# Two expert layers whose first nine slots are written among the routing of the last 20 tiles

## The chip, the cores and the metric

The kernel runs on one core of one Trainium2 chip. The metric is the device time in microseconds of one execution, taken as the median of several. TensorE does products and turns (transposes), VectorE, ScalarE and GpSimd the elementwise work, SyncE issues most transfers. A pass is one weight load with its stream: a product in f32 is recorded as two of them.

## What is computed

4096 tokens of width 256 (4 sequences of 1024) go through two layers. The part that matters here is the first layer:

```python
x = x + 0.5 * _L0_ffn_ref(_layernorm(x, axis=-1), ...)     # experts, first time
x = x + _L0_attn_ref(_layernorm(x, axis=-1), ...)          # causal attention, 16 heads of 16
x = x + 0.5 * _L0_ffn_ref(_layernorm(x, axis=-1), ...)     # experts, second time
x = x + 0.5 * _L1_ffn_ref(...)                             # block-wise quantized feed-forward
x = x + _L1_attn_ref(...)                                  # linear attention
x = x + 0.5 * _L1_ffn_ref(...)

def _L0_ffn_ref(hidden_states, W_router, W1, b1, Wo, bo, ln_gamma, ln_beta):
    logits = x @ W_router                                  # 4 experts
    expert_idx = jnp.argmax(logits, axis=-1)               # each token takes one
    h = gelu(jnp.einsum('th,ehi->tei', x, W1) + b1)        # 256 -> 1024
    intermediate = jnp.einsum('te,tei->ti', onehot, h)
    y = intermediate @ Wo + bo + x                         # 1024 -> 256
    return _layer_norm(y, ln_gamma, ln_beta)
```

## The kernel before

**Tiles and slots.** The tokens stand in 32 tiles of 128 rows. So that a token meets one expert alone, each layer of experts first routes: it normalizes all tiles, finds each token's expert, and scatters the tokens into `sorted_x` in DRAM, one region of rows for each expert. The experts then work on slots of 128 rows of one region; 35 slots (`SLOTS` = 32 + 3) hold any division of the tokens. A table says for each slot which expert it has (`expert_of`) and which row it starts at (`row_of`); SyncE and VectorE read it as registers. Results go to `sorted_y` and are gathered back tile by tile.

**Phases.** `build` (L2163) runs setup, `route_phase` (r0), `expert_qkv_phase`, `attention_phase`, `route_phase` (r1) and `second_layer_phase` one after the other, each with its own block and an all-engine barrier at its end. r1 also does the output projection of attention ahead of the norm; its fp4 weights are loaded meanwhile.

**Routing** (`route_phase`, L254). Stages are written as `(step, stage, every)`: stage k of tile t is issued at step t + k, in the same order on every engine, all unrolled. For tile t: turn_y L479 and project L486 (r1 only), join L329 on VectorE adds the projection to X; for four tiles measure L340 to L348; GpSimd takes the root L462; take_shift L355; ScalarE normalizes L437; TensorE turns L494; ScalarE evacuates L443; TensorE's router L503 gives four logits; choose L371 to L381 on VectorE, for four tiles; count_up L514 to L522; put L390 to L394; GpSimd scatters one tile with an indirect transfer L468. Banks of PSUM: two each for turned tiles, logits and projections. After tile 31 the table of slots is made by turns between TensorE (L534 to L547) and VectorE (L403 to L423).

**Experts** (`experts`, L556). One step is one slot. SyncE: load L603 (slice of sorted_x), load_weights L608 (1 MB of w1), load_residual L612, store L616 (waits for the finished slot). TensorE: 14 warm-up products L156, then turn L632, up_proj L641, down_proj L650 of three slots in a row, into two banks for the turn, two pairs of banks for up, two banks for down. ScalarE: evacuate L660, eight Gelus L671. VectorE: quantize_weights L1338 to L1423 (in the second layer, 18 pieces, one a slot, turned by TensorE at L1430), take_bias L682, place_results L717 to L741 (once, 25 linked steps, gives the rows for the gather), finish L690 to L172, norm L188 of the slot before. GpSimd: root L754, scale L761 and L762, gather L776.

**What follows the experts.** In the first layer `queries_keys_values` (L799) is interleaved with them, in the second the feed-forward stage (L1472) and the rest. `interleave` (L99) merges parts by their place; events at the same place keep the order of the parts and then of the stages. All waits are explicit semaphores.

## Time and profile before

| | us |
|---|---|
| median of 3 runs (2191.99 to 2197.48) | 2192.93 |
| the profiled execution | 2192.66 |
| its span, first to last instruction | 2190.9 |
| TensorE busy | 2043.9 (93%) |
| VectorE busy | 1455.5 (66%) |
| ScalarE busy | 1020.9 (47%) |
| GpSimd busy | 923.1 (42%) |

The profile is of one execution. Matmuls are pipelined and their ends are modelled, so that a start of the next one says more than a duration. A row `x32 3.74` is 32 instructions joined. What stands in brackets behind a row is the idle time ahead of it on its engine and what ended it. PE is TensorE, PEld its weight loads, DVE VectorE, ACT ScalarE, POOL GpSimd, SPq SyncE's queue.

### The profile page before, as it was taken

Reading aid. Unit: us, or ns where it says so; the run is one execution under the profiler, and the core shown is the slowest. Engines: PE = TensorE matmul, PEld = TensorE weight load, DVE = VectorE, ACT = ScalarE, POOL = GpSimd, SP = SyncE. Lnnn points to the kernel's source line nnn. Section 1 sums busy time; section 2 is a strip of 40 time slices with the busy share of each in tenths; the row PEclk is TensorE's granted clock in tenths of the full one; section 3 lists DMA queues with packets and bytes.
Section 4 is the critical chain, followed back from the end, with each engine's and each line's share of the span. In section 5 each row is a group of like instructions: output and inputs, shape, how many; then the busy total and the mean of one; then the engine's idle time right before and its main releaser. Section 6 shows DMA issues by size and latency. Waiting matters only on the chain.

```text
span 2190.9 us, 41818 instructions
## 1 busy us (share of the span) xinstructions
PE 2043.9 (93%) x13713; PEld 1408.7 (64%) x13713; DVE 1455.5 (66%) x3982; ACT 1020.9 (47%) x2367; POOL 923.1 (42%) x1137
## 2 busy tenths in 40 slices
PE   6799999989999999978899998999989999799998
PEld 6688887534444444347798885666766666566676
DVE  5344345478888888626675248889866666588884
ACT  4333333426666666645333333333346666533332
POOL 5334445412111111216134346555546666455553
PEclk9999999969999999998999999999999999999999
DMA  5456663563344444111556652000000000000000
GB/s 172 153 197 208 212 208 122 156 99 48 48 58 59 60 58 50 13 41 71 177 199 206 211 193 61 1 0 0 1 1 2 2 2 2 1 10 10 19 20 19
DMA packets 101710, 173.57 MB, mean 79 GB/s; under 512 B 14705, under 2 KB 66321, under 8 KB 101521
## 3 DMA queue, kind: packets, MB, share of 16 engines
q1 hardware_dynamic: 95376, 154.40, 26.7%
q0 software_dynamic: 6144, 16.79, 2.5%
q8 instruction: 102, 1.67, 0.3%
q14 instruction: 88, 0.71, 0.1%
HBM read 136.01 MB, written 34.87 MB: 78 GB/s over the span
## 4 chain that ended last, share of the span: by engine, by line
PE 23%; issue 10%; DVE 10%; POOL 6%; ACT 2%; DVEq 0%; POOLq 0%; DMA 0%; ACTq 0%; SPq 0%
PE s_H L1645 6%; PE s_Y L1675 4%; PE s_H L1997 3%; PE s_H L1984 1%; DVE ff_hscale L1358 1%; PE s_TY L2032 1%; PE s_Y L2068 1%; PE s_Y L2076 1%; PE s_H L2018 1%; DVE fw_down L1361 1%; DVE s_H L1538 1%; POOL V L776 1%; POOL fw_down L1588 1%; POOL e_yo L761 1%; POOL e_rstd L754 1%
## 5 line engine op out<-in xcount | busy, mean ns | idle before, releaser
L1253 DVE TENSOR_REDUCE a_part_max<-a_psS 128x1 f32<-128x512 f32 (+3 forms) x608 | 362.6, 654 | 78.0 <-PE a_psS L1183 69.2
L1309 ACT ACTIVATE a_PT<-a_psE 128x512 f32<-128x512 f32 (+1 forms) x608 | 309.3, 583 | 177.6 <-PE a_psE L1197 160.7
L1158 POOL TENSOR_SCALAR_AFFINE_SELECT a_PT<-a_PT 128x512 f32<-128x512 f32 x128 | 81.5, 636 | 407.7 <-ACT a_PT L1309 407.7
L1177 PE MATMUL a_psS<-sk,sq 96*128 96x512 bf16 (+3 forms) x768 | 234.4, 342 | 11.9 <-DMA sk<-qk_parts 8.1
L1197 PE MATMUL a_psE<-sq,sk 98*128 98x512 bf16 (+3 forms) x768 | 224.6, 329 | 2.5 <-ACT a_PT L1309 1.4
L1588 POOL TENSOR_TENSOR fw_down<-fw_down,ff_hm 128x704 f32<-128x704 f32 x64 | 97.3, 1521 | 248.1 <-DVE fw_down L1370 248.1
L1675 PE MATMUL s_Y<-w_down,fw_up 128*128 128x256 f32 x768 | 181.0, 386 | 20.9 <-ACT fw_up L1625 19.2
L754 POOL TENSOR_TENSOR e_rstd<-e_moments,minus_half 128x1 f32<-128x1 f32 x70 | 45.5, 649 | 333.5 <-DVE e_moments L172 333.5
L1610 ACT ACTIVATE ff_hm<-fw_down 128x704 bf16<-128x704 f32 x64 | 50.6, 790 | 280.3 <-DVE fw_down L1361 280.3
L1675 PEld LDWEIGHTS s_Y<-w_down,fw_up 128*128 128x128 f32 x768 | 143.5, 191 | 46.1 <-ACT fw_up L1625 29.0
L1645 PE MATMUL s_H<-w_gate,ff_xqT 128*128 128x512 f32 (+1 forms) x512 | 165.4, 467 | 3.0 <-ACT ff_sil L1620 3.0
L1645 PE MATMUL s_H<-w_up,ff_xqT 128*128 128x512 f32 (+1 forms) x512 | 164.2, 464 | 3.6 <-DVE fw_down L1361 2.4
L1197 PEld LDWEIGHTS a_psE<-sq,sk 98*128 98x128 bf16 x768 | 70.6, 98 | 131.7 <-issue 50.4
L1213 PE MATMUL a_psO<-a_PT,a_va 128*32 128x512 f32 (+3 forms) x1536 | 150.4, 494 | 2.5 <-POOL a_PT L1158 1.8
L1645 PEld LDWEIGHTS s_H<-w_gate,ff_xqT 128*128 128x128 f32 x512 | 90.2, 193 | 66.5 <-issue 66.4
L1645 PEld LDWEIGHTS s_H<-w_up,ff_xqT 128*128 128x128 f32 x512 | 89.6, 192 | 66.6 <-issue 61.9
L641 PE MATMUL eq_H<-e_xsT,e_w 128*128 128x128 f32 x1120 | 130.8, 275 | 0.0
L641 PE MATMUL s_H<-e_xsT,e_w 128*128 128x128 f32 x1120 | 130.8, 275 | 0.0
L1177 PEld LDWEIGHTS a_psS<-sk,sq 96*128 96x128 bf16 x768 | 73.0, 99 | 89.2 <-DVE a_part_max L1253 52.0
L641 PEld LDWEIGHTS eq_H<-e_xsT,e_w 128*128 128x128 f32 x1120 | 127.9, 192 | 0.1
L641 PEld LDWEIGHTS s_H<-e_xsT,e_w 128*128 128x128 f32 x1120 | 127.9, 192 | 0.1
L650 PE MATMUL eq_Y<-wo_moe,e_gT 128*128 128x256 f32 x560 | 126.7, 379 | 0.0
(374 smaller groups left out, 4314.8 us busy)
## 6 DMA issues: line engine op xcount, KB each, us to landing
e_w<-w_in SPq DMA_DIRECT2D x70, 1024.0 KB, 4.9
sq<-qk_parts SPq DMA_DIRECT2D x96, 128.0 KB, 5.9
sk<-qk_parts SPq DMA_DIRECT2D x96, 128.0 KB, 6.5
e_xs<-sorted_x SPq DMA_DIRECT2D x70, 128.0 KB, 2.4
e_xr<-sorted_x SPq DMA_DIRECT2D x70, 128.0 KB, 4.1
sorted_y<-e_yo SPq DMA_DIRECT2D x70, 128.0 KB, 1.7
X<-x_in SPq DMA_DIRECT2D x8, 512.0 KB, 6.4
qk_parts<-q_hi SPq DMA_DIRECT2D x32, 128.0 KB, 1.7
```

Of the source, the lines that this page charges most:

```text
L641: mm = pe.matmul(psH[p][:, n * P:(n + 1) * P], w1[p][:, k, n * P:(n + 1) * P], xsT[p][:, k, :], start=k == 0, stop=k == KD - 1)
L650: mm = pe.matmul(psY[p][:, 0:D], gT[p][:, k, :], st.wo_moe[:, k, :], start=k == 0, stop=k == KI - 1)
L754: pool.tensor_tensor(rstd[p][:], moments[p][:, 1:2], st.minus_half[:], ALU.pow).then_inc(rooted, 1)
L1158: pool.affine_select(out=hidden, in_=hidden, compare_op=ALU.is_ge, fill=0.0, base=0, pattern=[[0, HG], [1, P]], channel_multiplier=-1).the ...
L1177: mm = pe.matmul(out[:, i * n:(i + 1) * n], sq[it % 3][0:SROWS, h0 + i, qt * P:(qt + 1) * P], sk[it % 3][0:SROWS, h0 + i, c * 512:c * 512 ...
L1197: mm = pe.matmul(out[:, i * n:(i + 1) * n], sk[it % 3][0:KROW, h0 + i, kt * P:(kt + 1) * P], sq[it % 3][0:KROW, h0 + i, q0:q0 + n], start= ...
L1213: mm = pe.matmul(psO[32 * h:32 * h + 32, q0:(c + 1) * 512], va[it % 2][:, kt, h, :], PT[kt % 2][:, h, q0:(c + 1) * 512], start=kt == 0, st ...
L1253: dve.tensor_reduce(part_max[:, c, h0:h0 + heads, qt], psS[place % RING][:, 0:heads * n].rearrange("p (h k) -> p h k", h=heads), AX.X, ALU ...
L1309: act.activation(PT[kt % 2][:, h0:h0 + heads, q0:q0 + n], psE[e % RING][:, 0:heads * n].rearrange("p (h q) -> p h q", h=heads), ACT.Exp, s ...
L1588: c.link(pool.tensor_tensor(hv[i], hv[i], hm[i][:], ALU.subtract))
L1645: mm = pe.matmul(out[:, a:b], xqT[p % 2][:, k, :], w[:, k, a:b], start=k == 0, stop=k == KD - 1)
L1675: mm = pe.matmul(psY[:, 0:D], hqT[p % 2][:, k, :], st.w_down[:, k, :], start=k == 0, stop=k == KF - 1)
```

## The change

It takes both routing phases into the programs of what follows them, as a part for `interleave`, at four routing steps a slot, beginning 6.5 (first layer) or 7.75 (second) slots ahead of slot 0. Positions below are slots in that order.

- Two tables of slots. After 12 tiles are chosen, a first table lists the full slots among them, at most nine. Slots 0 to 8 read it; they wait for the scatters of the first 12 tiles and not for the others. After tile 31 a second table lists the remaining slots; slots 9 to 34 read it. The table of numbers for the result rows is made from both. place_results goes from slot 1 to position 5.75.
- One bank each for routing's turned tiles, projections, and logits with ranks; one for the experts' turn, one for each half of up, one for down. So each is reused one tile or slot back and not two. The Gelu's semaphore counts halves. Up and down are issued in halves, routing between them. The 14 warm-up products are gone.
- Stages of the experts move: load and load_weights one slot earlier, load_residual from 2 to 1, down from 2 to 2.5 and 2.75, activate to 1.5, finish from 2 to 3, norm to 3.75, root to 3.5, scale to 4, store to 4.25; the gather and the norm behind it go by a function of the tile. The parts behind the experts start 0.25 to 1 slot later.
- The nine loads of small weights are waited for one by one. In attention two of three sq and sk buffers are made there, and GpSimd sets their spare rows; VectorE did it among the slots.

```diff
+FIRST_TILES = 12
+FIRST_SLOTS = FIRST_TILES - EXPERTS + 1
+STEPS = 4
+LEAD = FIRST_TILES + 14
...
+        def project(t, p):
+            pe.wait_ge(yevac, t + 1)
+            reuse(pe, joined, t, back=1)
...
+        def turn(t, p):
+            pe.wait_ge(normed, t + 1)
+            reuse(pe, evacuated, t, back=1)
...
+    def first_order_tensor(pe):
+
+        def count(t, p):
+            pe.wait_ge(choice, CHOICE * (FIRST_TILES // G))
...
+        return [(0, count), (1, add_up), (2, position), (3, list_slots)]
...
+        return [(0, take_counts), (1, fill), (2, mark), (3, tell)]
...
+        return [(0, count), (1, add_up), (2, position), (3, list_slots), (4, number)]
...
+        return [(0, take_counts), (1, begin), (2, mark), (3, tell), (4, take_numbers)]
...
+    pace = 1 / STEPS
+    start = -(J + LEAD) * pace
+    at = lambda step, stages: (start + step * pace, pace, 1, 1, False, stages)
+    main = lambda stages: (start, pace, TILES, G, False, stages)
+    FIRST_AT, LAST_AT, WEIGHTS_AT = J + FIRST_TILES + 7, J + TILES + 7, J + 12
...
+            if t in (0, FIRST_SLOTS):
+                sp.wait_ge(r.ordered, 2 * order_of(t) + 2)
+                sp.wait_ge(*(r.scattered if order_of(t) else r.scattered_first))
...
-        return [(0, load), (0, load_weights), (2, load_residual), (4, store)]
+        return [(-1, load), (-1, load_weights), (1, load_residual), (4.25, store)]
...
-        keep_warm(pe, psY[0], st, 14)
-
...
-            reuse(pe, evacuated, t)
+            reuse(pe, evacuated, t, back=1)
...
+        def up_proj(t, p, half):
+            if half == 0:
+                pe.wait_ge(evacuated, t + 1)
+                pe.wait_ge(w_in[p], 8 * (t - p) + 16)
+            if t >= 1:
+                pe.wait_ge(gelu, UP * (t - 1) + half + 1)
...
+        def down_proj(t, p, half):
+            if half == 0:
+                pe.wait_ge(gelu, UP * (t + 1))
+                if t == 0:
+                    pe.wait_ge(st.wo_loaded, 16)
+                if t >= 1:
+                    pe.wait_ge(out, OUT * (t - 1) + 1)
...
+        return [(0, turn), (1, lambda t, p: up_proj(t, p, 0)), (1.25, lambda t, p: up_proj(t, p, 1)),
+                (2.5, lambda t, p: down_proj(t, p, 0)), (2.75, lambda t, p: down_proj(t, p, 1))]
...
-        return [(0, evacuate), (1, activate)]
+        return [(0, evacuate), (1.5, activate)]
...
+        return ([(0, quantize_weights)] * (fp4 is not None) + [(0, take_bias), (r.done_at + 1, place_results), (3, finish),
+                (3.75, norm)] + [(3.75, set_spare_rows)] * (fp4 is None))
...
-        return [(0, root), (1, scale)]
+        return [(3.5, root), (4, scale)]
+
+    def fetch_at(t):
+        return max(FIRST_TILES + 7.25 + 0.5 * t, t + 8)
...
+            pool.wait_ge(v_set, 5)
+            for i in (1, 2):
+                pool.memset(sk[i][SROWS:P, :, :], 1.0).then_inc(spared, 1)
+                pool.wait_ge(spared, i)
```

## Rows read from the trace of the kernel before

**Rows 1.** Page, the 40 slices: busy tenths of TensorE.
```profile
PE   6799999989999999978899998999989999799998
```
**Rows 2.** Stretches: length, busy us of PE, PEld, DVE, ACT, POOL; clock, DMA share, GB/s.
```profile
10.00:62.00 52.00, 43.09 (x217) 40.18 (x217) 26.81 (x156) 26.66 (x61) 29.94 (x31) 1.00 0.48 163
...
74.00:86.40 12.40, 5.42 (x19) 2.27 (x20) 5.59 (x24) 0.38 (x1) 0.00 (x0) 1.00 0.43 156
```
**Rows 3.** Timeline of TensorE, last expert slots of the first layer: start, us, instruction.
```profile
325.56 0.44 PE L632 MATMUL eq_T<-ident,e_xs 128*128 128x128 f32 x2 [0.41 <-DMA e_xs<-sorted_x]
...
332.89 0.44 PE L632 MATMUL eq_T<-ident,e_xs 128*128 128x128 f32 x2
...
340.19 3.73 PE L641 MATMUL eq_H<-e_xsT,e_w 128*128 128x128 f32 x32
```
**Rows 4.** Timeline of all engines around the first slots of the first layer.
```profile
79.57 0.36 SPq L603 DMA_DIRECT2D e_xs<-sorted_x  x1
...
80.74 0.39 SPq L608 DMA_DIRECT2D e_w<-w_in  x1
...
86.39 3.74 PE L641 MATMUL eq_H<-e_xsT,e_w 128*128 128x128 f32 x32
...
90.18 3.74 PE L641 MATMUL eq_H<-e_xsT,e_w 128*128 128x128 f32 x32
```
**Rows 5.** Timeline of TensorE, first routing stage.
```profile
33.99 0.69 PE L494 MATMUL r_psT<-ident,normed_first 128*128 128x128 f32 x2 [0.31 <-ACT normed_first L437]
...
39.66 0.85 PE L503 MATMUL r_psL<-w_router,r_xnT 128*128 128x4 f32 x4
...
44.36 0.69 PE L494 MATMUL r_psT<-ident,normed_first 128*128 128x128 f32 x2 [0.31 <-ACT normed_first L437]
```
**Rows 6.** Timeline of TensorE, second routing stage and second layer of experts.
```profile
992.91 1.13 PE L486 MATMUL r_psA<-wo_attn,r_yT 128*128 128x256 f32 x4
...
994.31 0.51 PE L503 MATMUL r_psL<-w_router,r_xnT 128*128 128x4 f32 x4
994.73 1.13 PE L486 MATMUL r_psA<-wo_attn,r_yT 128*128 128x256 f32 x4
...
1015.78 1.13 PE L486 MATMUL r_psA<-wo_attn,r_yT 128*128 128x256 f32 x4
...
1056.16 3.74 PE L641 MATMUL s_H<-e_xsT,e_w 128*128 128x128 f32 x32
...
1311.13 3.73 PE L641 MATMUL s_H<-e_xsT,e_w 128*128 128x128 f32 x32
```
**Rows 7.** Timeline of GpSimd, the scatter of tile 11 in the first layer.
```profile
43.21 0.96 POOL L468 DMA_INDIRECT sorted_x<-normed_first,slot  x1 [0.30 <-issue]
```
**Rows 8.** Page, DMA issues: the second layer's scatter, its median us to landing last.
```profile
sorted_x<-V,slot POOLq DMA_INDIRECT x32, 2.4
```
**Rows 9.** Timeline of VectorE, first and last step of place_results, first layer.
```profile
80.47 0.59 DVE L717 TENSOR_TENSOR_SCAN latest<-ones,begun 128x32 f32<-128x32 f32 x4
...
87.07 0.19 DVE L741 SCALAR_TENSOR_TENSOR result_row<-e_rows,place 128x32 uint32<-128x32 f32 x1
```
**Rows 10.** Timeline of VectorE, second routing: first step of put, next join after measure.
```profile
996.65 0.17 DVE L390 TENSOR_TENSOR r_rank<-r_psN,region_f 128x16 f32<-128x16 f32 x1 [0.33 <-PE r_psN L522]
...
999.33 0.97 DVE L329 TENSOR_TENSOR X<-r_psA,X 128x256 f32<-128x256 f32 x2
```
**Rows 11.** Timeline of VectorE in a slot with a weight piece: finish, quantize's first and last.
```profile
1105.49 0.42 DVE L690 TENSOR_TENSOR e_y<-s_Y,e_xr 128x256 f32<-128x256 f32 x1 [1.15 <-PE s_Y L650]
...
1107.48 0.41 DVE L1338 TENSOR_REDUCE fw_scale<-fw_up 128x16 f32<-128x256 f32 x1
...
1110.99 0.43 DVE L1423 TENSOR_TENSOR fw_up<-fw_v,fw_scale 128x256 f32<-128x256 f32 x1
```
**Rows 12.** ScalarE: loads at the Gelu line (duration, first and last start); an Identity in time.
```profile
L671 ACT ACT_TABLE_LOAD  x2: 1283/1283/1283, 88.4 to 1058.2; - x2
...
1295.87 0.58 ACT L1601 ACTIVATE ff_xn<-X,ff_shift,ff_rstd 128x256 f32<-128x256 f32 x1
```

More of the change, by code:

```diff
@@ L102, in step @@
-    def step(order, s, phase, static):
-        _, n, unroll, _, stages = placed[order]
-        for k, stage, *every in stages:
-            p = (phase - k) % unroll
-            if (not static or 0 <= s - k < n) and (not every or (s - k) % every[0] == 0 if static else not every or p % every[0] == 0):
-                stage(s - k, p)
-    for _, order, s, tail in sorted(events, key=lambda e: e[:3]):
-        unroll = placed[order][2]
+        head = tail
+        if loop:
+            ends = [o[0] + o[1] * step_of(g[0], o[2] - 1) for o in placed[:order] for g in o[5]]
+            first = max(max(g[0] for g in stages) + 2, *((end - start) / pace for end in ends), 0)
+            head = int(-(-first // unroll)) * unroll
+            assert head < tail and all(start + pace * tail <= o[0] for o in placed[order + 1:])
+            events.append((start + pace * head, order, -1, head, tail))
@@ L111, in interleave @@
+        for which, (depth, stage, *every) in enumerate(stages):
+            for i in range(n):
+                step = step_of(depth, i)
+                if (not every or i % every[0] == 0) and not head <= step < tail or not loop and (not every or i % every[0] == 0):
+                    events.append((start + pace * step, order, which, i, None))
+    for _, order, which, i, tail in sorted(events, key=lambda e: e[:4]):
+        _, _, _, unroll, _, stages = placed[order]
         if tail is None:
-            step(order, s, s % unroll, True)
+            stages[which][1](i, i % unroll)
@@ L113, in interleave @@
         else:
-            with eng.Fori(s, tail - unroll + 1, unroll) as r:
+            with eng.Fori(i, tail - unroll + 1, unroll) as r:
                 for u in range(unroll):
-                    step(order, r + u if u else r, u, False)
+                    for depth, stage, *every in stages:
+                        p = (u - depth) % unroll
+                        if not every or p % every[0] == 0:
+                            stage((r + u if u else r) - depth, p)
 def reuse(eng, sem, t, per=1, back=2):
```

808 lines of the change are left out of this document (449 added, 359 removed).

## Prediction, made before the change was run

> **What bounds the kernel now.** I read the 40 slices first, then a table of stretches, then TensorE's own rows stage by stage, and last the other engines' rows where TensorE waits. The slices show TensorE busy at 0.8 or more nearly everywhere; the dips that this change can reach are slices 1 and 2 (0.6, 0.7) and 18 to 20 (0.7, 0.8, 0.8) [rows 1]. These are the two routing stages. In the first one TensorE is busy 43.1 of 52 us, then 5.4 of 12.4 us, most of that the 14 warm-up products, before the first expert product [rows 2]. The expert stages that follow are bound by TensorE: a slot is one turn, 16 up products and 16 half-width down passes, back to back, 7.33 us (325.56 to 332.89), and a slice that lands late adds 0.41 us in front of it [rows 3]. From up product 1 at 90.18 to that of slot 34 at 340.19 a slot takes 7.58 us [rows 3, 4], so 0.25 us a slot is lost, and late slices are the one wait that the rows show.
>
> **The first routing stage now.** From the turn of tile 14 (33.99) to that of tile 20 (44.36) a tile takes 1.73 us, with TensorE waiting 0.31 us for ScalarE's normalized tile at each; a router group costs 0.85 us where the same group costs 0.51 us in the second stage [rows 5, 6]. So the first stage runs at TensorE's lower level (1.2 GHz), although the clock column prints 1.00 there [rows 2]; I go by durations. The first up product starts at 86.39 [rows 4].
>
> **The change, step by step.** A position is one slot in the written order of every engine, a routing step a quarter of one; routing step 26 (turn of tile 21) falls on position 0. Whatever TensorE does before it is the old sequence.
> (1) *Arrival at position 0.* Old time 44.36 plus one tile, 46.1 [rows 5]. The first table of slots puts four small products and fifteen VectorE steps in front. VectorE also puts places and measures in that step; TensorE waits for both. I take 2.5 us (0 if ScalarE's loop hides them, 5 if each of four hops is exposed): 48.6.
> (2) *Can slot 0 start there?* Its slice needs the scatters of 12 tiles. Scatter 8 to 11 end at 44.2 [rows 7]; the router now goes ahead of the count and the table's copy ahead of the placing, 1.2 us later: 45.4. The scatter lands 2.4 us later [rows 8], SyncE reads a register and issues, 1.1 us (the step between its issues at 79.57 and 80.74 [rows 4]), and the slice takes about another 2.4: 51.3. TensorE thus stands about 2.7 us, and ScalarE behind it, since its evacuation of slot 0 is next in its order. VectorE's bias of slot 0 waits for the same table; it has nothing queued that is due sooner.
> (3) *Position 0 to 1.* Four tiles at 1.64 to 1.73 us and a turn: 7 us, so the first up product starts at 58.3. Its weights are asked for 1.2 us behind the slice, at 50.1, and took at most 5.65 us before (80.74 to 86.39) [rows 4]: no wait. Gained at this point: 86.4 - 58.3 = 28.1 us. Two block ends and the 14 warm-up products lie in the stretch that goes.
> (4) *What is still owed.* Eight router groups of 0.42 (994.31 to 994.73, at the full level [rows 6]), seven turns of half as many passes, 0.21, and, as estimates, three counts of 0.5 and the second table at 1: 7.4 us of TensorE time that now lies among the slots. First slots at the lower level: 2 us. The second table's hops among slots 3 and 4: VectorE's chain of 12 steps against two half products, 1 to 3 us, taken at 1.5. The result rows, 25 steps from 80.47 to 87.26, 6.8 us on VectorE [rows 9], now come at position 5.75; the one down bank gives 3.8 us of patience (turn and up), so about 0.5 us shows.
> (5) *Every slot.* The slice is now loaded one slot earlier, ahead of the blocked wait for the store. That takes the late slices away: 33 x 0.25 = 8 us in each layer.
> The first layer: 28.1 - 7.4 - 2 - 1.5 - 0.5 + 8.3 = 25 us less (16 to 31).
>
> **The second routing stage** also does the output projection, and there the banks matter. Before, a tile takes 1.82 us (992.91 to 994.73) [rows 6] at two projection banks. With one, project(t+1) waits until VectorE has added tile t. Where VectorE places and measures four tiles (996.65 to 999.33, 2.7 us [rows 10]), the add stands behind it: 2.7 + 0.45 + 0.1 against 1.82 gives 1.4 us. Four such steps, three with the measuring alone (0.7 each) and four choices (0.2 each) cost 8.5 us up to position 0. The first table sits in the same queue: VectorE waits in it for TensorE, and the next projection waits for VectorE; 1.1 + 1.6 + 1.9 + 1.3 = 6 us for its four steps. At position 0 VectorE first quantizes a weight piece (1107.48 to 1111.42, 3.9 us [rows 11]) plus clears and bias, 5.2 us, ahead of the add that projection 30 waits for. Old time of projection 30, 1015.78 [rows 6], + 8.5 + 6 + 5.2 = 1035.5, and four tiles, 7 us, give the first up product at 1042.5. It was 1056.16: 13.7 us gained.
> Owed: 7.4 us as above. Then VectorE. In a slot with a weight piece it finishes (1105.49 to about 1107.24, 1.75 us), now waits about 0.8 us for GpSimd's root of the same slot instead of taking the one before, normalizes 0.4, quantizes 3.9 and loads a bias 0.5: 7.4 us [rows 11] beside 7.5 of TensorE. It has no room. The choices, second table and result rows (1.4 + 0.8 + 6.5 + 6.8) therefore come through, less the 4.8 us of patience: walking the queue I find waits of 1.1, 0.5, 3.5 and 4.3 us, 9.4 in all. Slots: the first up product follows the one before it without a down product between (3.8 us at 86.39 and 90.18 [rows 4]), so (1311.13 - 1056.16 - 3.8)/33 = 7.61 us before [rows 6]; 7.33, and 0.22 more for 18 of them, after: about 6 us gained of 8. The second layer: 13.7 - 7.4 - 9.4 + 6 = 3 us less (-10 to +20).
>
> **The sum.** The profiled execution took 2192.66 us, its span 2190.9, so 1.8 us lie around it; the median of the runs is 2192.93, the same for this purpose. 2192.7 - 25 - 3 = 2164.7; I add 1.3 us for the deeper pipe at the two ends of the expert stages (0 to 3): **2166.0**. Edits at nothing: the spare rows on GpSimd in attention, whose memsets (32 x 4096) lie ahead of its first masks and are wanted one batch later; the q start one slot later, with its groups long normalized; new names of banks in the feed-forward stages, same sizes. If the memsets were not hidden, under 10 us.
>
> **The rivals.**
> *A, the forecast*, 2145 to 2180: first layer gains much, second little.
> *B, VectorE is not so rigid*: the second stage gains like the first. Without the 14.5 us of projection waits and with 4 instead of 9.4: 2166 - 20 = 2146, down to 2140. For it: VectorE is busy only 26.8 of 52 us in the first routing stage [rows 2]. Against: those waits are of order, not of load.
> *C, slower*: **one bank for the down product ties the slots to VectorE**. TensorE may start down(t+1) only when VectorE took down(t). Without the 14 us of step (5) in the two layers the change gains 13; it turns slower once a slot lasts 7.6 + 13/66 = 7.8 us. VectorE's 7.4 us would have to be 0.4 us longer for all slots, or 0.8 in the 18 with pieces and some in the others. At 8.2 us a slot: 66 x 0.6 = 40 - 13, so 2192.7 + 27 = 2220. Against: in the first layer VectorE waits for the product, not the reverse. The Trainium skill's "PSUM — Partial Sum Buffer", "Summary: rules for kernel authors", says to read one bank while products run in another; the change keeps to that between products, but not from one slot to the next, and no row of before shows that state.
> *D, it doesn't overlap*: slice 0 comes so late that routing stands until it does. Then only the block ends and step (5) are left: about 12 us in all, 2181 to 2190, middle 2186.
> *E, ScalarE reloads tables* between Identity and Gelu: some 6 loads of 1.28 us a layer, 15 us: 2180. Against: only two loads stand at the Gelu line, at 88.4 and 1058.2, though an Identity of the feed-forward stage runs at 1295.87 among later Gelus [rows 12].
> *F, TensorE stays at its lower level.* The warm-up products go; the up products ran at the full level from 86.39 on, 32 passes in 3.74 us [rows 4], and now start in a stage whose router groups cost 0.85 us [rows 5]. Low through slots 0 to 3 they take twice 7.3 us, 27 us above my 2: 2193. Against: from position 1 on the work is unbroken. The Trainium skill's "TensorE: Matmul & The Clock Gate", section "What's actually happening", has an idle array fall back to half rate and sustained work raise it: it speaks for F where TensorE stands at slot 0, and against it behind.
>
> **How the numbers follow.** A 0.53, B 0.16, D 0.11, C 0.09, E 0.06, F 0.05. The range goes from near B's end to D's, 2143 to 2190, leaving out C, F and the tails of the others, 2 in 10. A measurement of this kernel tells about 0.3% from no change, 6.6 us: faster, below 2186.1, holds A, B, E and half of D, 0.81; the same holds the rest of D, F and a little of C, 0.11; slower 0.08.
>
> **What would show it.** The first up product of layer one at 56 to 61 us, of layer two 10 to 17 us ahead of old; router groups of 0.5 us among slots; no wait for e_xs in steady slots and slots of 7.3 us; TensorE waiting for VectorE at the projection, and at the down product in slots 3 to 7 of layer two only. Wrong if slots of layer one are above 7.5 us, or if TensorE stands over 6 us at the first slice.

## The result, and the profile of the changed kernel

The changed kernel takes 2176.2 us in the median (2174.6 to 2178.3) beside 2195.2 for the kernel before (2192.0 to 2197.5) in the same session: ratio 0.9915, 95% interval 0.9896 to 0.9934. That is 19 us less; the forecast was 27 less (2166.0), with 2176 inside its range. The profiled execution has a span of 2173.4 us where the one before had 2190.9, 17.5 less.

The page of the changed kernel, its head and its slices, to be held against [rows 1]:

```profile
span 2173.4 us, 41823 instructions
PE 2031.1 (93%) x13717; PEld 1414.7 (65%) x13717; DVE 1467.3 (68%) x4020; ACT 1018.7 (47%) x2367; POOL 922.0 (42%) x1139
PE   6899999899999999977899998999989999799998
PEclk9899999969999999998999999999999999999999
```

Slice 2, at 0.7 before, is now 0.8, and the dip of slices 18 to 20 has moved little. The slices can't show more. The stretches that answer to [rows 2] (length; busy us of PE, PEld, DVE, ACT, POOL; clock; DMA share; GB/s):

```profile
10.00:62.00 52.00, 41.78 (x211) 37.61 (x212) 27.35 (x164) 23.36 (x55) 25.58 (x26) 1.00 0.61 200
74.00:86.40 12.40, 12.40 (x100) 11.93 (x100) 3.72 (x19) 5.60 (x18) 4.60 (x5) 0.97 0.42 150
```

The stretch from 74 to 86.4, in which TensorE did little but the 14 warm-up products before, is full. But look at TensorE's rows among the first slots of layer one (start, us, instruction, and in brackets the idle time before it and what ended it):

```profile
50.86 0.69 PE L773 MATMUL b_T<-ident,e_xs 128*128 128x128 f32 x2 [2.97 <-DMA e_xs<-sorted_x]
...
57.94 3.49 PE L785 MATMUL b_H<-e_xsT,e_w 128*128 128x128 f32 x16
...
61.85 2.03 PE L785 MATMUL b_H<-e_xsT,e_w 128*128 128x128 f32 x16
...
69.30 0.69 PE L460 MATMUL b_RT<-ident,V 128*128 128x128 f32 x2 [3.46 <-ACT V L407]
69.78 0.85 PE L471 MATMUL b_RL<-w_router,r_xnT 128*128 128x4 f32 x4
...
70.95 3.62 PE L785 MATMUL b_H<-e_xsT,e_w 128*128 128x128 f32 x16
...
96.25 0.28 PE L585 MATMUL b_RA<-r_is_slot,expert_col 128*1 128x35 f32 x2 [2.93 <-DVE r_numbers L628]
...
97.26 3.62 PE L785 MATMUL b_H<-e_xsT,e_w 128*128 128x128 f32 x16
```

Slot 0 is turned at 50.86 after a wait of 2.97 us and multiplied from 57.94 (the forecast said 51.3, 2.7 and 58.3). Then two waits follow that the forecast did not have, 3.46 us for ScalarE and 2.93 us for VectorE, and behind each the next half of the up products (70.95, 97.26) takes 3.62 us instead of 1.95 to 2.03, TensorE's lower level against its full one; the first half of slot 0 (57.94) takes 3.49.

What stands ahead of those two waits in the other engines' queues. ScalarE, then VectorE:

```profile
65.02 1.28 ACT L821 ACT_TABLE_LOAD   x1
66.32 2.17 ACT L821 ACTIVATE e_gT<-b_H,e_bias 128x128 f32<-128x128 f32 x8
68.33 0.43 ACT L413 ACTIVATE r_xnT<-b_RT 128x256 f32<-128x256 f32 x1
68.59 0.66 ACT L407 ACTIVATE V<-X,r_shift,r_rstd 128x256 f32<-128x256 f32 x1
```

```profile
92.17 3.47 DVE L860 MEMSET sk<- 32x4096 bf16 x1 [0.91 <-issue]
95.66 0.30 DVE L627 TENSOR_SCALAR r_is_slot<-slot_number_f,b_RA,r_flag 128x35 f32<-128x35 f32 x1
95.88 0.31 DVE L628 TENSOR_SCALAR r_numbers<-ident_bf,b_RA,r_flag 128x128 bf16<-128x128 bf16 x1
```

The normalized tile waits behind a table load and eight Gelus; the mark of the second table waits behind a memset of spare rows that the change left on VectorE.

In layer two the rows that answer to [rows 6], then TensorE's waits in its routing and first slots (us in all, times, longest):

```profile
1014.48 2.04 PE L452 MATMUL s_R<-wo_attn,ff_sil 128*128 128x256 f32 x4 [3.09 <-DVE X L333]
...
1017.88 2.06 PE L452 MATMUL s_R<-wo_attn,ff_sil 128*128 128x256 f32 x4
...
1024.68 0.63 PE L773 MATMUL s_T<-ident,e_xs 128*128 128x128 f32 x2
...
1066.45 0.23 PE L593 MATMUL s_R<-r_numbers,ones_bf 128*128 128x128 bf16 x1 [3.11 <-DVE r_match_bf L640]
...
1086.19 3.69 PE L797 MATMUL s_Y<-wo_moe,e_gT 128*128 128x256 f32 x16 [2.54 <-DVE e_y L844]
```

```profile
PE s_R L452 <- DVE X L333: 15.5, 11, 3.1
PE s_R L460 <- ACT V L407: 3.7, 2, 3.5
```

The stage now begins 17.5 us earlier (956.76 before, 939.25 after). The first up product starts at 1025.10, so 31.1 - 17.5 = 13.6 us are gained inside the stage, 13.7 in the forecast. The projection's wait for VectorE's addition, rival B's subject, is there: 15.5 us. Behind the first up product come the wait of 3.5 us for ScalarE once more, one of 3.11 us in the second table and one of 2.54 us at a down product.

To compare kernels I use one set of marks in us: the starts of the up products of slot 4 and of the last slot (34) of layer one, the mean distance between them, and in layer two the time from the start of projection 0 to the last slot's up product.

| kernel | slot 4, layer one | slot 34 | us a slot | layer two, projection 0 to slot 34 |
|---|---|---|---|---|
| before | 112.3 | 340.2 | 7.60 | 353.2 |
| changed | 105.4 | 322.6 | 7.24 | 354.9 |

This is the surprise. At the first up product the change is 28.4 us ahead; four slots later only 6.9 of them are left. The next thirty slots bring 10.7. In layer two the first up product is 13.6 us ahead on the stage's own clock; at slot 4 (1083.19 before, 1072.45 after) the change is 6.8 us behind, thirty slots bring 5.1, and it ends 1.7 behind. So up to slot 4 the two layers together have gained 0.1 us, and the gain stands in the steady slots behind it, 15.8 us. The question for the runs was therefore: what do the steady slots gain from, and where do the 21.5 us of layer one go?

### The profile page after: what moved, and what is told of

Its sections match the earlier page's. It is cut to its first block, busy times and chain, and to the rows that moved or that the text cites. A ratio compares the mean times of both kernels' runs of the same rounds, so it can differ in the third digit from the quotient of the medians.

```text
span 2173.4 us, 41823 instructions
## 1 busy us (share of the span) xinstructions
PE 2031.1 (93%) x13717; PEld 1414.7 (65%) x13717; DVE 1467.3 (68%) x4020; ACT 1018.7 (47%) x2367; POOL 922.0 (42%) x1139
## 3 DMA queue, kind: packets, MB, share of 16 engines
q8 instruction: 102, 1.67, 0.3%
## 4 chain that ended last, share of the span: by engine, by line
PE 35%; DVE 11%; issue 5%; POOL 2%; ACT 2%; DVEq 0%; DMA 0%; POOLq 0%; SPq 0%; ACTq 0%
PE s_HH L785 5%; PE s_Y L797 4%; PE s_Y L1851 4%; PE s_R L1821 3%; PE s_HH L1821 3%; PE s_HH L2173 3%; PE s_R L2160 1%; PE s_R L452 1%; PE s_R L2208 1%; PE s_Y L2244 1%; PE s_Y L2252 1%; PE s_R L2194 1%; DVE ff_hscale L1534 1%; DVE fw_down L1537 1%; DVE s_HH L1714 1%
## 5 line engine op out<-in xcount | busy, mean ns | idle before, releaser
L1821 PE MATMUL s_R<-w_gate,ff_xqT 128*128 128x512 f32 (+1 forms) x512 | 164.6, 465 | 4.8 <-ACT ff_sil L1796 4.8
L1821 PE MATMUL s_HH<-w_up,ff_xqT 128*128 128x512 f32 (+1 forms) x512 | 163.0, 462 | 3.6 <-DVE fw_down L1537 2.4
L1351 PE MATMUL a_psS<-a_sk,a_sq 96*128 96x512 bf16 (+2 forms) x480 | 144.0, 335 | 1.9 <-DVE a_part_max L1429 0.3
L1373 PE MATMUL a_psE<-a_sq,a_sk 98*128 98x512 bf16 (+3 forms) x480 | 140.6, 328 | 0.0
L785 PE MATMUL b_H<-e_xsT,e_w 128*128 128x128 f32 x1120 | 136.3, 281 | 0.0
L1821 PEld LDWEIGHTS s_R<-w_gate,ff_xqT 128*128 128x128 f32 x512 | 90.1, 193 | 67.4 <-issue 67.3
L797 PE MATMUL s_Y<-wo_moe,e_gT 128*128 128x256 f32 x560 | 129.2, 384 | 4.4 <-DVE e_y L844 2.5
L785 PE MATMUL s_HH<-e_xsT,e_w 128*128 128x128 f32 x1120 | 133.3, 278 | 0.0
L785 PEld LDWEIGHTS b_H<-e_xsT,e_w 128*128 128x128 f32 x1120 | 133.1, 198 | 0.1
L785 PEld LDWEIGHTS s_HH<-e_xsT,e_w 128*128 128x128 f32 x1120 | 130.3, 195 | 0.1
L797 PE MATMUL b_Y<-wo_moe,e_gT 128*128 128x256 f32 x560 | 127.8, 381 | 0.0
L797 PEld LDWEIGHTS s_Y<-wo_moe,e_gT 128*128 128x128 f32 x560 | 104.9, 193 | 17.8 <-issue 2.7
```

The source lines that it names most:

```text
L785: mm = pe.matmul(psH[half][:, n * P:(n + 1) * P], w1[p][:, k, c * P:(c + 1) * P], xsT[p][:, k, :], start=k == 0, stop=k == KD - 1)
L797: mm = pe.matmul(psY[:, 0:D], gT[p][:, k, :], st.wo_moe[:, k, :], start=k == 0, stop=k == KI - 1, skip_group_check=True)
L1351: mm = pe.matmul(out[:, i * n:(i + 1) * n], sq[it % 3][0:SROWS, h0 + i, qt * P:(qt + 1) * P], sk[it % 3][0:SROWS, h0 + i, c * 512:c * 512 ...
L1373: mm = pe.matmul(out[:, i * n:(i + 1) * n], sk[it % 3][0:KROW, h0 + i, kt * P:(kt + 1) * P], sq[it % 3][0:KROW, h0 + i, q0:q0 + n], start= ...
L1821: mm = pe.matmul(out[:, a:b], xqT[p % 2][:, k, :], w[:, k, a:b], start=k == 0, stop=k == KD - 1)
```

## The experiments

Ratios are to the kernel before, measured beside each run; the changed kernel's is 0.9915 (0.9896 to 0.9934). All marks are as above, of one profiled execution each; a table of them stands behind the last run.

**1. The memset of the spare rows later.**

```diff
-                (3.75, norm)] + [(3.75, set_spare_rows)] * (fp4 is None))
+                (3.75, norm)] + [(7.75, set_spare_rows)] * (fp4 is None))
```

> The changed kernel with one edit: the memset of the spare rows of sk on VectorE (3.47 us in its trace) runs four positions later, after both tables. Theory (two queue-order waits and the clock that they cost make up the 10 us that the forecast lacks in the first layer): TensorE's wait of 2.93 us for is_slot2 in the second table shrinks to under 1 us, the two instructions behind it come back from 3.62 to about 1.95 us (an up half) and from 4.19 to about 2.2 us (down), and the first layer is 4 to 6 us shorter; ratio to the kernel before about 0.989. Rival (the thirteen chained VectorE steps of the second table are themselves too long): the wait stays above 2 us, gain under 1 us. Rival (the granted clock does not hang on that wait): the wait goes but both durations stay, gain about 2.5 us.

Ratio 0.9913 (0.9896 to 0.9929). Slot 4 at 99.1 instead of 105.4, span 2169.2, 4.2 us less than the changed kernel's; layer two, which the edit does not touch, took 356.6 us in this profile instead of 354.9. Slot 3's rows:

```profile
90.61 1.95 PE L785 MATMUL b_H<-e_xsT,e_w 128*128 128x128 f32 x16
92.49 0.22 PE L585 MATMUL b_RA<-r_is_slot,expert_col 128*1 128x35 f32 x2
...
93.22 1.95 PE L785 MATMUL b_H<-e_xsT,e_w 128*128 128x128 f32 x16
```

The wait is gone and both halves run at the full level: 6.3 us at slot 4, of which 2.9 are the wait. The cause of that wait is shown. That the level came back by this edit is not: in runs 3, 4 and 8 the wait stands and the half behind it takes 1.95 us all the same. The whole kernel's gain, 0 to 4 us, can't be told from none by its median.

**2. The Gelus behind the routed tile.**

```diff
-        return [(0, evacuate), (1.5, activate)]
+        return [(0, evacuate), (1.6, activate)]
```

> The changed kernel with one edit: the Gelus of a slot stand at position 1.6 and not 1.5, so that ScalarE does the norm and the evacuation of the routed tiles of that step first. Theory: the waits of 3.46 us for ScalarE in the turn of the route tile, one in each layer, fall below 1 us, and the up half behind each goes from 3.62 to about 1.95 us; 4 us less in each layer, ratio to the kernel before about 0.988. Rival: the Gelus are late instead, and the down product or the next slot's turn waits the same time: nothing gained in total. Rival (clock does not hang on it): 2.5 us a layer.

Ratio 0.9912 (0.9896 to 0.9929). The wait of 3.46 us goes in both layers, and this comes in its place:

```profile
68.26 3.75 PE L785 MATMUL b_H<-e_xsT,e_w 128*128 128x128 f32 x16 [1.37 <-ACT e_gT L821]
```

Slot 4 at 103.8, 1.6 us sooner; layer two 354.9, unchanged. The rival was right in the main: TensorE now waits for the Gelus (1.37 us here, 0.66 in layer two), so ScalarE's queue is short of time there, not merely in the wrong order.

**3. TensorE kept busy ahead of slot 0.** Added ahead of the turn of slot 0, in both layers:

```diff
+            if isinstance(t, int) and t == 0:
+                for _ in range(14):
+                    pe.matmul(psH[0][:, 0:512], st.ident_bf[:], st.hide_k_after_q[:].unsqueeze(1).broadcast_to([P, 4, P]),
+                              start=True, stop=True)
```

> The changed kernel with 14 products of 512 columns in bfloat16 on TensorE ahead of the turn of slot 0 in both layers, written to a bank that is not in use yet; they compute nothing that is needed. They fill the wait of 2.97 us for the first rows. Theory (TensorE comes out of that wait at its lower level): the two up halves of slot 0 (3.49 us each at first) take about 1.95 us, the products themselves cost at most 0.5 us, and 1.5 to 3 us are gained in each layer, ratio about 0.990. Rival (the clock is set by the whole mixed stage and its short tiles, not by that wait): halves stay at 3.5 us and the added products cost up to 1 us a layer. If the profile shows the up halves at 1.95 and nothing gained, the time is lost again at the next wait for ScalarE.

Ratio 0.9913 (0.9895 to 0.9931). In layer one it does what it should:

```profile
57.99 0.42 PE L777 MATMUL b_T<-ident,e_xs 128*128 128x128 f32 x2
58.24 1.95 PE L789 MATMUL b_H<-e_xsT,e_w 128*128 128x128 f32 x16
60.77 2.03 PE L789 MATMUL b_H<-e_xsT,e_w 128*128 128x128 f32 x16
```

Slot 1 is then 1.1 us sooner than in the changed kernel (0.6 to 0.7 sooner than in runs 1 and 4, where the first half happened to take 2.9 us without help), but the same wait of 3.47 us for ScalarE follows at 68.2, and slot 1's first half takes 3.25 us. Slot 4 stands at 101.6, mostly because the half behind the second table's wait ran in 1.95 us this time. In layer two the first half took 3.32 us in spite of the added products. No gain shows in the median: the level at slot 0 is worth about 1 us.

**4. The loads one position later again.**

```diff
-        return [(-1, load), (-1, load_weights), (1, load_residual), (4.25, store)]
+        return [(0, load), (0, load_weights), (1, load_residual), (4.25, store)]
```

> The changed kernel with the loads of the slot's rows and weights at position 0 again, as in the kernel before, and not at -1. Theory of the forecast's step 5: the steady slots of the first layer go from 7.25 back to about 7.58 us, with a wait of about 0.4 us at each slot's turn for the rows; 7 to 9 us more in the first layer and 4 to 8 in the second, ratio about 0.998. Rival (the slot was shortened by the new position of the Gelus or the banks and not by the loads): slots stay at 7.25 us, ratio 0.9915.

Ratio 0.9957 (0.9941 to 0.9972), 9 us more than the changed kernel, clear of both intervals, but not for the reason given. Steady slots keep their 7.25 us. TensorE waits for late rows twice in layer one, 1.81 us at slot 9, the first of the second table, and 0.59 us at 286.8, and 1.84 us at slot 9 of layer two:

```profile
118.82 0.44 PE L773 MATMUL b_T<-ident,e_xs 128*128 128x128 f32 x2 [1.81 <-DMA e_xs<-sorted_x]
```

From slot 4 to slot 34 of layer one that is 220.5 us, where the changed kernel takes 217.2 and the kernel before 227.9. **So the shorter slot does not need the load at -1**, to which the forecast's step 5 gave it. Layer two takes 362.4 us instead of 354.9: 1.84 is the wait at slot 9, 2.4 one for r_hit at 1032 (0.6 in the changed kernel), 3.5 a longer projection stretch, 81.0 us against 77.5. Of these 3.5, 2.5 lie ahead of projection 5, where four products took 2.07 us each, the lower level, and only two in the changed kernel. Run 1 had the wait for r_hit too, with its loads at -1, so part of this difference varies from profile to profile, and how much of the 9 us the loads cost is open.

**5. Before, with the normalizing right behind the finish.** If not the loads, then what shortens a slot? In the kernel before, SyncE waits here, and TensorE there (150 to 320):

```profile
SPq L616 <- POOL e_yo L762: 85.1, 22, 4.6
...
PE eq_T L632 <- DMA e_xs<-sorted_x: 5.7, 11, 0.9
```

The store stands in SyncE's queue ahead of the next slot's load and waits for the scaled rows. One slot of the kernel before:

```profile
202.56 0.42 DVE L690 TENSOR_TENSOR e_y<-eq_Y,e_xr 128x256 f32<-128x256 f32 x1 [4.86 <-PE eq_Y L650]
204.23 0.41 DVE L188 TENSOR_SCALAR e_y<-e_y,e_moments,e_rstd 128x256 f32<-128x256 f32 x1
205.85 0.73 POOL L762 TENSOR_TENSOR e_yo<-e_yo,beta 128x256 f32<-128x256 f32 x1
206.61 0.33 SPq L616 DMA_DIRECT2D sorted_y<-e_yo  x1
207.69 0.34 SPq L603 DMA_DIRECT2D e_xs<-sorted_x  x1
210.26 0.44 PE L632 MATMUL eq_T<-ident,e_xs 128*128 128x128 f32 x2
```

VectorE normalizes a slot (204.23) only behind the next slot's finish (202.56), a whole slot late. GpSimd ends at 206.58, the store goes at 206.61, the load at 207.69, and TensorE wants the rows at 210.26, 2.57 us later, where such a load lands 2.4 us after its issue in the median of that profile. The change also put the normalizing 0.75 of a position behind the finish instead of one. Done alone, on the kernel before:

```diff
-        (0, take_bias), (1, place_results), (2, finish), (3, norm)]
+        (0, take_bias), (1, place_results), (2, finish), (2, norm)]
-        return [(0, root), (1, scale)]
+        return [(0, root), (0, scale)]
```

> The kernel before with one edit: VectorE normalizes a slot right behind its finish, not one slot later, and GpSimd scales it right behind. Theory N (the 0.25 to 0.33 us that a steady slot lost came from the store, which waited for the scaled rows and held up the next slot's load behind it): SyncE no longer waits 85 us for e_yo in 150 to 320, TensorE's waits for e_xs go, steady slots fall from 7.58 to about 7.3 us and the kernel is 15 to 20 us shorter, ratio about 0.992, as much as the whole change. Rival (the half-width down products, the early Gelus or the single banks of the change make the slot shorter): slots stay at 7.58 us, ratio 1.000. Rival (VectorE now waits for GpSimd's root inside the slot and has no room in the 18 slots with weight pieces): first layer 8 to 10 us less, second layer up to 8 us more.

Ratio **0.9922** (0.9909 to 0.9936), which the noise can't tell from the whole change's. In 150 to 320 SyncE's wait for the scaled rows falls to 3.8 us, and a wait that costs nothing takes its place:

```profile
SPq L607 <- PE eq_H L641: 76.3, 24, 3.4
SPq L616 <- POOL e_yo L762: 3.8, 6, 1.0
```

Here the load goes at 207.04 for a turn at about 214.1, 7 us ahead, and in 150 to 320 TensorE waits for no rows. Slot 4 at 112.8, slot 34 at 330.0, 7.24 us a slot, 10.2 us less than before from slot 4 on. Layer two 350.3, only 3.0 less; but the projections, which the edit doesn't touch, took 63.9 us in this profile against 59.7. Behind the last projection it is 286.4 against 293.5, 7 us less, and 10.2 and 7 make the 17 us of the median.

**6. The changed kernel with the old order of normalizing.** With the loads at position 0 as in 4:

```diff
-                (3.75, norm)]
+                (4, norm)]
```

> The changed kernel with the loads at position 0 and the normalizing of a slot one slot later (position 4 instead of 3.75, so behind the next slot's finish), both as in the kernel before. Theory N: steady slots go back to about 7.58 us with a wait of 0.3 us for e_xs at the turns, some 15 us more than with the loads at 0 alone, ratio about 1.002. Rival (something else than this order shortens the slots): slots stay at 7.25 us and the ratio at 0.996.

Ratio 1.0006 (0.9996 to 1.0017): the whole gain of the change is gone, although the overlap, the banks and the two tables are all there. 7.61 us a slot; the late rows are back, and in 150 to 320 the store waits for the scaled rows 23.9 us, 3.8 in run 4:

```profile
SPq L758 <- POOL e_yo L921: 23.9, 22, 1.8
...
287.34 0.44 PE L773 MATMUL b_T<-ident,e_xs 128*128 128x128 f32 x2 [1.02 <-DMA e_xs<-sorted_x]
```

Between runs 4 and 6 only the normalizing differs: 7.35 and 7.61 us a slot, slot 34 of layer one 10.0 us later, 11 us in the medians. Layer two differs little, 362.0 us in run 6 and 362.4 in run 4; behind the last projection it is 284.3 against 281.5.

Runs 5 and 6 settle that the order of normalizing shortens the slot by itself, on either kernel, as long as the load stands at 0. What no run shows is the changed kernel with the old order and the load at -1, the forecast's own cause alone. By the rows of before such a load would go some 10 us ahead of its turn, as an estimate (2.57 and a slot of 7.6), where 2.4 are needed: it may well suffice too. The change makes both edits, and either can be the one that counts in it.

**7. The changed kernel without overlap.**

```diff
-LEAD = FIRST_TILES + 14
+LEAD = TILES + 14
```

> The changed kernel with slot 0 at a position behind the whole routing (the lead of the routing raised from 26 to 46 steps), so that no routing step lies among the slots; one program, both tables, banks and the order inside a slot stay. Theory S (the overlap as such is worth little, since the routing steps cost nearly as much among the slots as alone, and the gain is that of the steady slots): slot 4 of layer one starts its up product within 5 us of 105.4, and in layer two within 8 us of 1072.5; ratio 0.988 to 0.995. Rival O (the overlap carries the gain, as the forecast had it, 28 us in the first layer less 11): 15 to 20 us more in the first layer, 5 to 15 in the second, ratio about 1.002. In both cases the waits of 3.5 us for ScalarE and of 2.9 and 3.1 us in the second table go.

Ratio 0.9961 (0.9947 to 0.9975), so the overlap as such is worth 10 us (2184.5 - 2174.4 at the before median of 2193.0). The first up product stands at 80.2, so 6.2 of the 28.4 us gained at that place come without overlap (block ends and warm-up products are gone here too). Slot 4 of layer one at 108.3, 2.9 us later than with overlap; layer two 361.0, 6.1 more. That lies between the two theories: the overlap pays, but of the 22 us by which it brings forward layer one's first product only 2.9 are left at slot 4.

**8. The weight piece quantized later.**

```diff
-        return ([(0, quantize_weights)] * (fp4 is not None) + ...
+        return ([(0.6, quantize_weights)] * (fp4 is not None) + ...
```

> The changed kernel with one edit: in layer two VectorE quantizes a slot's weight piece at position 0.6 of the slot and not at 0, so for the first slot behind the last addition of a projected tile. Theory (the wait of 3.09 us at the projection at 1014.5 is the quantizing of the first piece ahead of that addition): that wait falls to about 0.8 us and the first up product of layer two comes 2 to 3 us sooner; total 0 to 3 us less. Rival (VectorE has no room from there on, so the piece is only late somewhere else): a wait of the same size appears at fp4's turn or at the down product in slots 1 to 4, total unchanged or up to 5 us more.

Ratio 0.9932 (0.9917 to 0.9948). The wait of 3.09 us goes, and one of 4.87 us for the quantized piece appears at the turn at 1026.2, another of 3.25 at 1064.0: layer two 361.2 instead of 354.9. The rival holds: VectorE has no room there.

**9. Without overlap, two projection banks.** As run 7, and in layer two (psP holds routing's bank for projections and the first up bank, which is free until slot 0):

```diff
-            dve.tensor_tensor(st.X[:, t, :], psA[:, 0:D], st.X[:, t, :], ALU.add).then_inc(joined, 1)
+            dve.tensor_tensor(st.X[:, t, :], psP[p % 2][:, 0:D], st.X[:, t, :], ALU.add).then_inc(joined, 1)
-            reuse(pe, joined, t, back=1)
+            reuse(pe, joined, t, back=2)
-                mm = pe.matmul(psA[:, 0:D], yT[p % 2][:, k, :], st.wo_attn[:, k, :],
+                mm = pe.matmul(psP[p % 2][:, 0:D], yT[p % 2][:, k, :], st.wo_attn[:, k, :],
```

> The changed kernel with all routing ahead of slot 0, as in the run without overlap, and with two banks instead of one for the output projection of layer two (the second is the first up bank, which is free until slot 0). Theory (the waits for X at the projection, 11.8 us in the nine of 0.8 us or more in the run without overlap, come from the single bank: project(t+1) stands until VectorE has added tile t): they go to under 2 us, projection 0 to 31 takes 60 to 64 us instead of 72.6, and the ratio falls from 0.996 to 0.991 to 0.993. Rival (VectorE has too much to do there, so that the wait only moves to the router or the counts): the stretch stays above 70 us and the ratio at 0.996.

Ratio 0.9905 (0.9888 to 0.9921). TensorE's longest waits in 935 to 1062, first two of run 7, then one of this run, in which no wait for the addition is over 0.4 us:

```profile
PE s_R L452 <- DVE X L333: 12.4, 10, 1.9
PE s_T L1606 <- DVE fw_gate L1599: 8.0, 2, 4.2
```

```profile
PE s_T L1606 <- DVE fw_gate L1599: 9.1, 2, 4.9
```

Projection 0 to 31 takes 60.6 us instead of 72.6, layer two 348.0 instead of 361.0. One bank costs 12 us, more than the 6 that overlap brings in that layer. The Trainium skill's "PSUM — Partial Sum Buffer", "Summary: rules for kernel authors", says to target a different bank where PSUM is read while a product runs. With one bank this kernel can only wait instead, and this pair of runs gives the price of that, 12 us over 32 tiles.

**10. A candidate.** Layer one with overlap and run 1's memset; layer two as in run 9; and

```diff
-        return ([(0, quantize_weights)] * (fp4 is not None) + ...
+        return ([(-0.2, quantize_weights)] * (fp4 is not None) + ...
```

> A candidate. Layer one: the changed kernel's overlap, with the memset of the spare rows on VectorE four positions later. Layer two: no overlap, two projection banks, and each weight piece quantized 0.2 positions sooner, so that the first is done while slot 0 waits for its rows. Expected from the runs so far against the changed kernel: layer one 6 us less up to slot 4 (4 of them in the span); layer two, from projection 0 to the last up product, 361.0 us without overlap, less 9 to 12 for the banks and less 4 to 7 for the two waits of 4.2 and 3.8 us for quantized pieces: 342 to 348 against 354.9. In all 10 to 17 us less than the changed kernel, ratio to the kernel before 0.984 to 0.987. If overlap and banks aren't additive like this (a finish later by the quantizing of 3.9 us, which then holds up the store), 0.990.

2164.0 us in the median, ratio **0.9863** (0.9847 to 0.9880): below both kernels by more than the intervals, 11 us below the changed one. Slot 4 at 101.0, layer two 348.0, as in run 9. The sooner quantizing brought nothing: TensorE still waits at slots 1 and 2.

```profile
1028.90 0.66 PE L1606 MATMUL s_T<-ident,fw_gate 128*128 128x128 f32 x2 [4.19 <-DVE fw_gate L1599]
1039.48 0.66 PE L1606 MATMUL s_T<-ident,fw_gate 128*128 128x128 f32 x2 [4.92 <-DVE fw_gate L1599]
```

**11. Three routing steps to a slot, with the late memset.** STEPS = 3 for STEPS = 4.

> The changed kernel with the late memset and with three routing steps to a slot instead of four, in both layers. Theory (the waits among the first slots come from four tiles and a table squeezed beside one slot on ScalarE and VectorE): the wait of 3.47 us for the normalized tile in slot 1 falls below 2 us and the later steps of the second table find VectorE free; 2 to 5 us less than with the late memset alone, ratio 0.989. Rival (order decides, not density: the norm still stands behind eight Gelus): the same wait of 3.5 us once in each layer, total unchanged at 0.991.

Ratio 0.9907 (0.9891 to 0.9924), the same as run 1. The wait for the normalized tile does go; a Gelu is waited for 1.16 us, the result rows hold up a down product for 2.95 us at 124.1, and in layer two the second table waits 4.12 and a down product 4.76 us. The waits change places, and the time stays.

**12. The candidate with the pieces one slot later.** The piece turned in slot t is t - 2, and the count of pieces that the turn waits for moves with it:

```diff
-        return t - 1 if fp4 and 1 <= t <= len(fp4.pieces) else None
+        return t - 2 if fp4 and 2 <= t <= len(fp4.pieces) + 1 else None
```

> The candidate of the run h1 with one more edit: slot t of layer two turns weight piece t-2 and not t-1, so that the first piece is due at the turn of slot 2. In h1 TensorE waits 4.19 and 4.92 us for quantized pieces at slots 1 and 2. Theory (VectorE starts on the first piece only after the last table, and one slot more of distance covers it): the two waits shrink to under 2 us together, 6 to 8 us less, ratio about 0.983. Rival (VectorE is the engine that sets the pace of these first slots, which are 3.8 us apart on TensorE and hold 3.9 us of quantizing and 1.75 of finishing each): the wait moves to the down product of slots 1 to 3 and the gain is under 3 us, ratio 0.985.

Ratio 0.9860 (0.9838 to 0.9882), no different from run 10. Both waits for pieces are gone, 9.1 us, and of the gain 0.6 is left from the last projection to slot 4 (66.8 against 67.4 us). TensorE's longest waits in 1035 to 1065 are now:

```profile
PE s_Y L797 <- DVE e_y L844: 3.0, 1, 3.0
PE s_R L593 <- DVE r_match_bf L640: 1.4, 1, 1.4
PE s_HH L785 <- ACT e_gT L821: 1.4, 2, 1.0
```

The first and the last of them are new, 4.4 us together; the middle one, of the last table, run 10 has too. Another of 2.52 us, again for VectorE, is new at 1024.4, ahead of slot 0. The rival holds again.

This profile's projection stretch, the same code as in run 10, took 68.0 us instead of 60.6. Of the 7.4 us, 3.3 lie ahead of projection 5: four products of 2.07 us each, where run 10 has one of 2.07, one of 1.67 and then 1.13 us; the granted clock in 940 to 950 was 0.54 in this run and 1.00 in run 10. The other 4 us are open. The kernel before, measured beside this run, also took 8 us longer than beside run 10, 2202.6 us in the median against 2194.6.

All marks, in the order of the runs:

| run | ratio | slot 4, layer one | slot 34 | us a slot | layer two, projection 0 to slot 34 |
|---|---|---|---|---|---|
| 1, memset later | 0.9913 | 99.1 | 316.3 | 7.24 | 356.6 |
| 2, Gelus later | 0.9912 | 103.8 | 321.0 | 7.24 | 354.9 |
| 3, TensorE kept busy | 0.9913 | 101.6 | 318.8 | 7.24 | 356.6 |
| 4, loads at 0 | 0.9957 | 102.6 | 323.1 | 7.35 | 362.4 |
| 5, before with normalizing behind the finish | 0.9922 | 112.8 | 330.0 | 7.24 | 350.3 |
| 6, changed with the old order, loads at 0 | 1.0006 | 104.9 | 333.1 | 7.61 | 362.0 |
| 7, no overlap | 0.9961 | 108.3 | 325.5 | 7.24 | 361.0 |
| 8, pieces quantized later | 0.9932 | 103.1 | 320.3 | 7.24 | 361.2 |
| 9, no overlap, two banks | 0.9905 | 108.3 | 325.5 | 7.24 | 348.0 |
| 10, candidate | 0.9863 | 101.0 | 318.2 | 7.24 | 348.0 |
| 11, three steps a slot | 0.9907 | 93.9 | 317.6 | 7.46 | 356.0 |
| 12, candidate, pieces a slot later | 0.9860 | 100.8 | 318.0 | 7.24 | 355.0 |

## Why the prediction was right, and where it was not

Sign, size and range held, but in part by luck. The forecast had 13.6 us from the starts of the two layers (28.1 - 11.4 and 13.7 - 16.8) and 14.3 from their steady slots (8.3 and 6). Up to slot 4 the change brought 0.1 us and behind it 15.8: overlapping brought nothing net of its costs, the single bank among them, and the number held because the steady slots came out well, where the forecast did not have the cause that the runs show.

**Steps 1 to 3 held.** Turn of slot 0 at 50.86 (51.3), a stand of 2.97 us (2.7), first up product at 57.94 (58.3), gain 28.4 us (28.1). Reading the old order up to position 0 and adding hop for hop from measured rows was enough.

**Step 4 was mis-sized: 11.4 us owed, 21.5 measured at slot 4.** Two waits, 3.46 and 2.93 us, stand where 1.5 was put down for the second table. And the lower level was priced at 2 us: the halves at 57.94, 70.95 and 97.26 alone take 3.49, 3.62 and 3.62 us where 1.95 is the full level, 4.9 us more, and routers and a down product come on top. Run 1 shows one of the two waits, 2.9 us for a memset of 3.47; the 3.3 us of lower level behind it came and went without that edit too. The forecast put all spare rows on GpSimd; one memset stayed on VectorE, and it was in the diff. The other wait is ScalarE's, which the forecast looked at for table loads alone (rival E) and not for its queue: one load and eight Gelus, 3.5 us, ahead of a tile that TensorE wants.

**Step 5 had the right size and overlooked a cause.** 8.3 us forecast, 10.7 measured from slot 4 to 34. The forecast credited the load at position -1, past the blocked store. Run 4 takes that away and all but 3.3 us of it stay: the store is no longer blocked, because the normalizing of a slot comes ahead of the next finish (runs 5 and 6). That the load at -1 would not have done alone is not shown. I had seen that the load stood behind the store [rows 4] and did not ask what the store waited for; the answer, 85.1 us on GpSimd's scaled rows, was one view of SyncE's waits away.

**Layer two: the stage held, the first slots didn't.** Projection 30 came 16.2 us later than before on the stage's own clock (1014.48 + 17.5 - 1015.78), 19.7 forecast; the first up product was right within 0.2 us. Rival B's subject, the stalls at the projection, is real: 15.5 us measured, and 12 us come back with a second bank (run 9). Behind that the forecast had 7.4 + 9.4 us owed and 6 gained by the slots (its own figures, 33 slots from 7.61 to 7.33 with 0.22 more for 18 of them, give 5.3). Measured are 20.4 us lost from slot 0 to slot 4 and 5.1 gained from there on; the layer ended 1.7 us behind instead of 3 ahead. Of the 9.4 us of waits for VectorE, 6.3 came: 0.64 for r_hit, 3.11 in the second table, 2.54 at a down product. The wait of 3.46 us for ScalarE came on top, and halves at the lower level again.

**The sum.** Layer one 17.6 instead of 25, layer two -1.7 instead of 3: 12.1 us short. The 1.3 us for the pipe's ends did not show, and 1.6 us were gained behind the second layer: 9.2 short, 26.7 against 17.5 in the span.

**The rivals.** A is what happened by its number. B did not occur: its waits at the projection are there, and VectorE is as rigid as feared in the first slots (runs 8 and 12 each removed a wait for it and found it again elsewhere; in run 2 it was ScalarE). The projection's waits themselves are a matter of the bank, as run 9 shows. C did not occur: steady slots are 7.24 us in layer one and 7.47 (1090.16 to 1097.63) with weight pieces in layer two, where it asked for 7.8. D did not occur, slot 0 came on time. Its price, about 12 us, was too low by the forecast's own terms, as step 5 alone has 14 in two layers; run 7, with no overlap at all, came to 2184.5, inside D's 2181 to 2190. E did not occur: two table loads at the Gelu line, one a layer, as in [rows 12]. F in part: not through all of slots 0 to 3, but 5 us and more where 2 were priced; its remedy at slot 0 gave about 1 us (run 3).

What the change is worth, by parts: the order of normalizing about 17 us on the kernel before (run 5) and 11 on the changed one with its loads at 0 (run 6 against 4), the overlap about 10 (run 7), the loads at -1 about 9 (run 4, its cause in part open), and the single projection bank takes 12 back in layer two (run 9 against 7: 2184.5 - 2172.2). These were measured on different kernels, the first and the third overlap, and they need not add up.

## What to carry to other kernels

When a diff rewrites a schedule, ask which small order in it frees the steady loop: here one stage moved from behind the next slot's finish to ahead of it, on an engine that was never the bound of the steady slots, was worth about as much by itself as the whole change. Where a change makes two edits that could each free the loop, run each without the other before naming the one that did. Follow each late transfer back through its queue, to what the instruction ahead of it waits for, before crediting an edit. And before overlapping two stages, list for each engine what is queued ahead of the first thing that the bounding engine wants: an overlap gives back at such places what it gained, and where one engine is full, as VectorE was in runs 8 and 12, moving its work only moves the wait.

## What the runs showed of the hardware

TensorE's level after a wait was not the same from profile to profile. Behind the wait of 2.9 us in the second table of layer one, the same 16 passes at the same place took 3.62 us in the changed kernel and in run 2 and 1.95 us in runs 3, 4 and 8. Run 8 differs from the changed kernel in layer two alone, so up to there the two are one program:

```profile
97.26 3.62 PE L785 MATMUL b_H<-e_xsT,e_w 128*128 128x128 f32 x16
```

```profile
96.27 1.95 PE L785 MATMUL b_H<-e_xsT,e_w 128*128 128x128 f32 x16
96.83 1.95 PE L785 MATMUL b_H<-e_xsT,e_w 128*128 128x128 f32 x16
```

(The first is the changed kernel's, the others are those of runs 4 and 8.) So this wait of 3 us cost 3 us in some profiles and about 6 in others, and nothing in the program decided which. A mark of one profile can't carry a reading of 2 or 3 us by itself. The Trainium skill's "TensorE: Matmul & The Clock Gate", "What's actually happening", says that the number of slow products at the start of a kernel differs from run to run of one kernel; these rows show the same in the middle of one. It also calls the cost of the ramp under 1% of a typical kernel's span, and the 4.9 us of the three slow halves above, of 2173, are within that.
